# Sixteen-wide attention heads: the products of values and probabilities issued two quarters at a time, behind every second head

## The reference

```python
qh, kh, vh = heads(q @ wq), heads(k @ wk), heads(v @ wv)   # (4, 16, 512, 16)
scores = einsum('bhqd,bhkd->bhqk', qh, kh)                 # 512 x 512 for each of 64 (batch, head)
# layer 0 alone: scores where the mask is 0 are replaced by a large negative number
probs  = softmax(scores, axis=-1)
out    = einsum('bhqk,bhkd->bhqd', probs, vh)
x      = x + out.reshape(4, 512, 256) @ wo
```

## Time and profile before

| | us |
|---|---|
| median of 3 runs | 3407.94 |
| lowest, highest | 3407.82, 3412.77 |
| the profiled execution, its own time | 3407.43 |
| its span | 3404.6 |
| PE busy of the span | 2789.2 |
| DVE busy | 1897.8 |
| ACT busy | 1757.9 |
| attention16 of L0x, from 97 to 398 | about 300 |
| attention16 of L2x, from 1663 to 1915 | about 252 |

### The profile page before, as it was taken

The page is one execution under the profiler, slowest core; times in us unless marked ns, Lnnn a source line. Parts: engine busy times, 40 slices in busy tenths (PEclk is TensorE's granted clock), DMA queues, the critical chain, the costliest instruction groups (busy, mean ns, idle before and its releaser), DMA issues. The chain is left out here.

```text
span 3404.6 us, 47988 instructions
## 1 busy us (share of the span) xinstructions
PE 2789.2 (82%) x14944; PEld 1556.1 (46%) x14944; DVE 1897.8 (56%) x4784; ACT 1757.9 (52%) x2884; POOL 851.1 (25%) x957
## 2 busy tenths in 40 slices
PE   6799849789999996657699789999667777777777
PEld 3233339644444453323222359997324433433443
DVE  5777621255555655005688521114598888888853
ACT  3566411146555553001477423331589888988953
POOL 4100020110000000002200030003467677777740
PEclk9899969899999998778799999999879999999988
DMA  4111146410000002881222239994500000000001
GB/s 163 44 53 50 54 153 221 163 64 1 1 1 1 1 1 92 351 364 60 71 57 62 79 143 348 344 347 151 170 15 12 18 25 10 25 19 10 25 22 52
DMA packets 161802, 326.75 MB, mean 96 GB/s; under 512 B 29408, under 2 KB 128481, under 8 KB 138209
## 3 DMA queue, kind: packets, MB, share of 16 engines
q1 hardware_dynamic: 150544, 301.64, 25.6%
q0 software_dynamic: 4608, 12.59, 1.1%
q10 hardware_dynamic: 6480, 10.49, 0.9%
HBM read 275.22 MB, written 49.28 MB: 95 GB/s over the span
## 5 line engine op out<-in xcount | busy, mean ns | idle before, releaser
L2898 DVE TENSOR_TENSOR_SCAN L3x_fade<-L3x_first_exp,L3x_scores 128x513 f32<-128x513 f32 x256 | 311.4, 1216 | 60.0 <-PE L3x_probs_tp L2708 49.8
L2779 POOL TENSOR_TENSOR L3x_fade<-L3x_fade,L3x_apart 128x1024 f32<-128x1024 f32 x128 | 279.2, 2181 | 190.3 <-DVE L3x_mx L2916 172.7
L2705 PE MATMUL L3x_probs_tp<-identity,L3x_fade 128*128 128x128 f32 x1024 | 165.8, 286 | 168.4 <-ACT L3x_probs_T L2844 144.4
L1254 ACT ACTIVATE L1x_probs<-L1x_scores,L1x_neg_max 128x512 f32<-128x512 f32 x256 | 173.8, 684 | 226.3 <-DVE L1x_neg_max L1308 226.3
L2705 PEld LDWEIGHTS L3x_probs_tp<-identity,L3x_fade 128*128 128x128 f32 x1024 | 116.4, 144 | 275.6 <-issue 145.5
L1308 DVE TENSOR_REDUCE L1x_neg_max<-L1x_scores 128x2 f32<-128x1024 f32 x128 | 156.7, 1224 | 142.8 <-PE L1x_scores L1143 142.8
L1596 ACT ACTIVATE L2f_hiddenT<-L2f_hidden_ps,L2f_b1s 128x128 f32<-128x128 f32 x320 | 100.2, 364 | 209.2 <-PE L2f_hidden_ps L1531 209.2
L2816 ACT ACTIVATE L3x_first_exp<-L3x_scores,L3x_nm 128x512 f32<-128x512 f32 x256 | 175.6, 686 | 58.9 <-DVE L3x_nm L2890 56.7
L781 DVE CUSTOM_DVE_ANT_0 L0x_masked_scores<-L0x_s,L0x_mask_q 128x512 f32<-128x512 f32 x256 | 167.0, 685 | 56.7 <-issue 56.5
L2824 ACT ACTIVATE L3x_fade<-L3x_fade,L3x_tiny,L3x_rl 128x512 f32<-128x512 f32 x256 | 194.4, 813 | 0.0
L776 DVE TENSOR_REDUCE L2x_neg_max<-L2x_s 128x1 f32<-128x512 f32 x256 | 164.6, 685 | 34.6 <-PE L2x_s L670 34.3
(11 more groups left out here) (530 smaller groups left out, 6211.7 us busy)
## 6 DMA issues: line engine op xcount, KB each, us to landing
L2f_w1s<-in_L_w SPq DMA_DIRECT2D x40, 1024.0 KB, 7.6
L2f_w2s<-in_L_w SPq DMA_DIRECT2D x40, 1024.0 KB, 6.4
L1f_w1s<-in_L_w SPq DMA_DIRECT2D x32, 1024.0 KB, 15.8
L1f_w2s<-in_L_w SPq DMA_DIRECT2D x32, 1024.0 KB, 10.6
L0f_w1s<-in_L_w SPq DMA_DIRECT2D x16, 1024.0 KB, 6.1
L0f_w2s<-in_L_w SPq DMA_DIRECT2D x16, 1024.0 KB, 5.2
L0x_q_stack<-L0x_q_parts SPq DMA_DIRECT2D x96, 64.0 KB, 2.6
L0x_k_stack<-L0x_k_parts SPq DMA_DIRECT2D x96, 64.0 KB, 2.7
```

Of the source, the lines that this page charges most:

```text
L1254: nc.scalar.activation(p[:, n % 3, h, :], s[:, n % 2, h, :], ACT.Exp, bias=nmax[:, n % 4, h:h + 1], accum_out=den[:, n % 4, h:h + 1]).then ...
L2705: nc.tensor.matmul(tp[:, kt, :], fz[:, f, kt * P:(kt + 1) * P], c.ident[:], start=(kt == 0), stop=False, is_transpose=True)
L2779: nc.gpsimd.tensor_tensor(fz[:, f:f + 2, 0:S], fz[:, f:f + 2, 0:S], w, ALU.mult).then_inc(y_done, 1)
L2898: nc.vector.tensor_tensor_scan(fz[:, f, :], ex[:, t, :], sA[:, t, 0:1].to_broadcast([P, S + 1]), 0.0, ALU.add, ALU.bypass).then_inc(f_done, 1)
```

## The change

```diff
@@ -729,7 +729,8 @@
                     shifted(u, i, 1)
                     if last > 2:
                         scores(u + 2, (i + 2) % 8, [2, 3])
-                    if not first:
+                    if not first and r % 2:
+                        weigh(g + (-1), q, r - 1)
                         weigh(g + (-1), q, r)
```

## The result

| | us |
|---|---|
| changed kernel, median of 4 runs | 3430.91 (3425.87 to 3432.72) |
| kernel before, 4 runs by now | 3409.40 (3407.82 to 3412.77) |
| ratio | 1.0059, 95% interval 1.0042 to 1.0077 |
| profiled execution, its own time and its span | 3425.87, 3423.3 |

By the ratio that is 20 us (14 to 26); the forecast was 11. The profiled execution is 18.4 us longer than that of before.

What follows compares the result with a forecast made beforehand. It took PE as the bound, with DVE's pace stopping short bodies. 14 groups x (0.20 + 0.54) = 10.4 us, plus 0.9 for the first weighing group, made +11.3 on 3407.43: 3419 us; range 3410 to 3430.

Steps and rivals of the forecast that it cites:

- D: Distance between `turn_max` starts over the rest of r = 2, one quarter less: -0.66 us in L0x, -0.59 in L2x.
- C: Distance between `turn_max` starts over the rest of r = 1, one quarter more: +0.86 us in L0x, +0.82 in L2x.
- The stall before quarter 0: PE's wait in B behind `normalise`, 0.99 us in L0x and 0.68 in L2x, forecast to go.
- B: Distance between `turn_max` starts over r = 0, with `normalise`, one quarter less: -0.86 us in L0x, -0.51 in L2x.
- B without gain: Rival: body r = 0 takes DVE's first-body pace plus all of `normalise`; 3439 us, chance 0.12 for 3427 to 3440.
- the turn of the loop: Every second B longer by 0.16 us in L0x, 0.11 in L2x; assumed to go, hidden in DVE's wait for PE.
- A: Distance between `turn_max` starts into a group, weighing r = 3 then `turn_o`, one quarter more: +0.86 us L0x, +0.82 L2x.
- The group of L0x: Sum of the changes of A, B, C and D in L0x: +0.86 - 0.86 + 0.86 - 0.66 = +0.20 us.
- PE's pace: Rival: short bodies run at PE's own pace, D gives the full 1.00; 3399 us, chance 0.07 for 3395 to 3402.
- The wash: Rival: `normalise` overlaps the long piece, say 0.3 us less in each B; 3410 us, chance 0.18 for 3408 to 3414.
- The 0.14: PE's saving in us per joined pair of quarters, 1.00 less 0.86; alone, over 60 pairs, 8 us in all.

Runs made afterwards that it cites:

- e6: Changed kernel (quarters in pairs) with the row maxima taken over half of the keys in both layers; 0.9894 against the kernel before, 3402.51 us.
- e4: Kernel before with only quarter 2 moved, to quarter 3, in both layers; ratio 1.0040 against the kernel before.
- e2: Kernel before with quarters in pairs in L2x alone, L0x unchanged; ratio 1.0054 against the kernel before.
- e9: Kernel before with all four quarters weighed in one piece at the end of body r = 3, both layers; ratio 1.0096.
- e7: Kernel before with only quarter 0 moved one step later, behind the first half of `shifted` at r = 1, joined to nothing; ratio 0.9950.
- e11: The same kernel as e7, run once more on another chip; ratio 0.9952, 3392.40 against 3406.23 us for the kernel before.
- e3: Kernel before with only quarter 0 moved, to quarter 1, in both layers; ratio 1.0057 against the kernel before.
- e1: Kernel before with quarters in pairs in L0x alone, L2x unchanged; ratio 1.0032 against the kernel before.
- e5: Kernel before, quarters one at a time, with the row maxima taken over half of the keys in both layers; ratio 0.9934, 3416.96 us.
- e8: Kernel before with quarter 0 behind the first half of `shifted` at r = 1, quarters 1 and 2 between score tiles at r = 2 and 3; ratio 0.9953.
- e10: Changed kernel's pairs, each placed behind the first half of `shifted` of bodies r = 1 and r = 3; ratio 1.0016 against the kernel before.

## Why the prediction was right, and what it left out

**Direction and mechanism: right.** The long bodies pay a quarter in full and the short ones are stopped by DVE. Every distance of L0x that the prediction named came out to 0.01 in at least every second group, D in both layers exactly as in the first bodies of before. A piece of two quarters runs 1.92 or 1.93 us, the forecast 1.92. DVE has no idle time in D of L2x and 1.46 us in C, forecast 1.4. The stall before quarter 0 is down from 26 to 2.3 us in all. e6, where shorter reductions turn the sign, and e4, where the wait isn't moved, show the cause; it isn't only argued. The reading of L2x's wait in B was right too, though the row names an exponential: in the kernel before, `normalise` ends at 1717.24 + 0.42 = 1717.66, 0.15 us before quarter 0 starts at 1717.81, and ACT's exponential of that time runs until 1717.82, past the start.

```profile
1716.80 1.02 ACT L858 ACTIVATE L2x_probs_T<-L2x_s 128x1024 f32<-128x1024 f32 x1
1717.24 0.42 DVE L818 TENSOR_TENSOR L2x_o_batch<-L2x_o_acc,L2x_recip_den 128x256 f32 x1 [0.56 <-DVE L2x_recip_den L810]
```

**The time: less well met than the mechanism.** By the ratio the changed kernel stands at 3428 us on the 3407.94 of the prediction; the median of its four runs is 3430.91. That is above 3415 to 3426, to which the prediction gave 0.63, and lies where it had put B without gain (3427 to 3440, 0.12), whose mechanism did not come: B lost what was forecast, all but the turn of the loop. It is at the upper end of the range of 3410 to 3430, and that it is not clearly beyond is partly luck, as some 3 us of falls of the clock had no term at all, and another execution could have had more of them or fewer.

**Size: 20 against 11.** The terms that were too small:

- *A and C of L2x.* Taken as +0.82, they are +0.92. In the kernel's first bodies, from which I had DVE's pace, all waits are against constants. In the loop DVE computes the wait's value between the parts and the next maximum. DVE in the unrolled part and in the loop of the changed kernel:

```profile
1687.94 0.17 DVE L798 TENSOR_TENSOR L2x_neg_max_parts<-L2x_neg_max,L2x_neg_max_parts 128x4 bf16<-128x4 f32 x1
1688.02 2.61 DVE L777 TENSOR_REDUCE L2x_neg_max<-L2x_s 128x1 f32<-128x512 f32 x4
```

```profile
1735.39 0.17 DVE L798 TENSOR_TENSOR L2x_neg_max_parts<-L2x_neg_max,L2x_neg_max_parts 128x4 bf16<-128x4 f32 x1
1735.56 2.51 DVE L777 TENSOR_REDUCE L2x_neg_max<-L2x_s 128x1 f32<-128x512 f32 x4
...
1739.95 0.69 DVE L777 TENSOR_REDUCE L2x_neg_max<-L2x_s 128x1 f32<-128x512 f32 x1 [1.46 <-PE L2x_s L670]
```

  From the start of the parts' last step to the next maximum it is 0.08 unrolled and 0.17 in the loop, 0.09 more, and then tile 3 of the scores and the piece behind it are that much late. The trace has the instructions: in the loop one that works on registers (L772) begins at 1735.40, and the wait behind it comes at 1735.50, 0.11 after the last step began; unrolled there is none, and the wait comes 0.01 after it. Before, DVE's 0.54 us of idle time at this place covered it. In the unrolled part of the same execution C is 4.35, the forecast 4.34, and A 4.79, as forecast. Twice 0.10 in the twelve groups of the loop: 2.4 us.

- *The turn of the loop.* I took it as hidden. It isn't: every second B is 4.57 and 3.66 instead of 4.41 and 3.55, and every second A of L0x 5.53. The group of L0x costs +0.33 and not +0.20: 1.8 us; in L2x 0.05 a group, 0.7 us.

- *The clock.* The prediction had no term for it. In the changed kernel it fell once within the loop of L2x and once in its tail; before, not once there. Busy time by engine ahead of the fall, in it and behind it, and the piece that ran in it:

```profile
1777.60:1781.00 3.40, 3.40 (x26) 1.46 (x18) 1.46 (x3) 2.51 (x4) 0.62 (x1) 1.00 0.47 139
1781.00:1784.50 3.50, 2.36 (x12) 0.67 (x10) 3.37 (x8) 2.46 (x4) 0.00 (x0) 0.99 0.16 50
1784.50:1787.90 3.40, 3.40 (x17) 0.63 (x17) 1.53 (x4) 0.68 (x1) 0.00 (x0) 0.50 0.00 0
1787.90:1791.30 3.40, 3.30 (x19) 1.05 (x15) 2.20 (x4) 2.37 (x3) 0.00 (x0) 1.00 0.00 0
```

```profile
1784.97 3.34 PE L706 MATMUL L2x_o_acc<-L2x_probs_T,L2x_v_unit 128*32 128x512 f32 x16
```

  The piece takes 3.34 us instead of 1.93, and that C is 6.08 instead of 4.45: 1.6 us. From the last `turn_max` to the end of L2x it is 14.24 us, with the other fall, and 12.55 in e2, which had the same order and no fall there: 1.7 us.

- *The end of the stages.* Behind the last `turn_max` the sum had +0.20 and +0.23 (an A and a D). It became 13.46 for 12.93 us in L0x and, without the fall, 12.55 for 11.69 in L2x: 1.0 us more than the sum.

11.3 + 2.4 + 1.8 + 0.7 + 3.3 + 1.0 = 20.5, the 20.5 of the two stages.

One bound was off without moving the sum: the prediction took PE's own pace of D in L0x as 3.13 (4.13 less 1.00). In e6, where PE doesn't wait, it is 3.03.

**Terms that held.** A and C of L0x +0.86; D -0.66 and -0.59; B -0.86 and -0.51 in the groups without the loop's turn. The chain that gave B, `normalise` on DVE's way, stands in the changed kernel as the sum had it: 1732.70 (L811, the reciprocal) to 1733.87 (the next maximum) is 1.17, the forecast 1.15.

**The rivals.** PE's pace (3399) fell with D; e9 refutes it. The wash needed B to lose 0.3 more; it lost less. B without gain (3439) did not come. The 0.14 that the prediction took from the rows as saved by a joined pair is 0.24 in L0x of e6 and nothing in L2x of e6. In the changed kernel D reads 3.47 and 2.93, DVE's length, so none of it reaches the time.

## What to carry to other kernels

Where two engines hand tiles to each other through two buffers, as here, extra work of one of them is better spread out, or put where it would stand waiting for the other: put together, it lengthened one body in full, and the other body was stopped by the partner's pace. Before joining pieces of work, look for the bodies that have none of it (here the first four): their length is what a body can fall to. Take those at the full clock: in L2x the first ones take 4.04 us, at a granted clock of 0.50 from 1668 to 1680, and only the last one takes the 2.93. And a stall behind one wait can be had for a move of one step (e7 and e11, 14 to 17 us), without what came with it here.

## What the runs showed that I had not expected

The granted clock fell in some orders of the same work and not in others. In L2x it stayed at 1.00 through the loop in the kernel before; in the changed kernel it fell to 0.50 for 3.4 us once in the loop and once behind it, in e2 twice, in e3 six times, and in e9 for 6.8 us, 6.8, 10.2 and 6.8. These four are the kernels whose body r = 0, the one with `normalise`, weighs nothing while the maxima have their full length, and in which PE stands up to 0.87 us for DVE there. In e1, e4, e5, e6, e7, e8, e10 and e11 it did not fall in L2x, though e4, e6 and e10 join quarters too; so it isn't uneven work as such. Each count is that of one execution. Each fall that I looked at in the loop, in the changed kernel and in e3, followed that body, but in many other groups the same body was followed by no fall. Nor did every stretch in which PE had little to do bring one: in L0x of the kernel before PE is busy 2.22 of 3.40 us at one place, with a wait of 1.18 us in it, and the clock stays at 1.00; and in L0x of the changed kernel, e1, e3 and e9 body r = 0 is just as empty, with waits up to 0.84 us, and the clock fell nowhere in the loop.

```profile
139.65:143.05 3.40, 2.22 (x15) 0.67 (x14) 2.77 (x11) 1.60 (x2) 1.04 (x1) 1.00 0.52 142
```

What decides is open. The Trainium skill, TensorE: Matmul & The Clock Gate, A second HAM failure mode: psum-queue depth-cycling, tells of a kernel in which TensorE's short idle times between groups of matmuls, as PSUM banks are cycled, make the clock go back and forth. This case agrees in so far as the L2x loops in which the clock fell had no wait of PE over 0.87 us; the same case shows waits of that kind without a fall, in L0x.
